# Row sends in growing groups, fewer side pieces ahead of two key operations, and an earlier load of the experts' first rows

## The chip, the cores and the metric

One core of a Trainium2 chip runs the whole program in one launch. The metric is the device time of an execution in microseconds (us). The engines are TensorE (PE; its weight loads are PEld), VectorE (DVE), ScalarE (ACT), GpSimd (POOL) and SyncE (SP, which here only issues transfers).

## The reference, cut to what matters

The model has two layers, each an attention followed by a mixture-of-experts block; x is 4 sequences of 1024 tokens of width 128.

```python
x = x + attn_a(layernorm(x))    # 16 heads of 64, softmax kernel features, then an ELU network of 512
x = x + ffn(layernorm(x))       # 160 experts, 8 for each token, inner width 64, and a shared expert
x = x + attn_b(layernorm(x))    # 16 heads of 8, causal
x = x + ffn(layernorm(x))

# inside attn_a: linear attention by random features
dash = einsum('bnhd,md->bnhm', data * dn, proj)
diag = sum(square(data), -1, keepdims=True) * dn * dn / 2
f    = ratio * (exp(dash - diag - max) + 1e-6)     # max per token (queries) or over all (keys)
kv   = einsum('bnhm,bnhd->bhmd', kf, v)

# inside ffn
top_w, top_idx = top_k(sigmoid(x @ router + bias), 8)
routed = sum over the 8 experts of weight * down(silu(gate(x)))
```

## The kernel before

**Order of the work.** A pass for the largest key comes first, then `attn_a` for the batches b = 0 to 3, each 1024 tokens in 8 tiles of 128 (TPB = 8). In the profile b = 1 runs from about 243 to 435 us, b = 2 to 640, b = 3 to 833. Then come the ELU network of batch 3 (`ffn_a`, f3), the routing of its tokens (`route`, m3, from 872 us), the experts of the first layer (`experts`, m, 926 to 1282), layer b, the last routing (`route`, n3, from 2248) and the experts of the second layer (`experts`, n, from 2302 to the end).

**A key tile of `attn_a`.** TensorE projects the keys of the tile (`psA`), their dash (`psB`, line 1020 for queries and its sibling for keys) and the values (line 992). ScalarE squares the keys (`a__sq`, line 1132), GpSimd adds the halves of the squares (`a__fold`, `fold_key_squares`, line 949), VectorE reduces them to `a__shift` (`key_square_sums`, line 804) and subtracts that from the dash into `a__arg` (`key_argument`, line 811), ScalarE takes the exponential, TensorE adds kf·v up. The eight query tiles follow: `query_peak` (line 815), `query_argument` (lines 820 and 826), and others.

**Side work on VectorE.** While batch b is in its attention, VectorE also finishes the network of batch b-1 and routes its tokens. That side work is a generator of pieces: first the ELU network's end and the norm of the expert input (lines 378 to 403; line 403 writes `g_xs`, the rows that go to the experts), then the router's scores, ranks and slots (up to line 659). `side(t, phase, count)` runs the next `count` pieces at three places of key tile t, by a table of numbers:

```python
for t in range(TPB):
    side(t, 0, PIECES[t][0])
    key_square_sums(t)
    side(t, 1, PIECES[t][1])
    key_argument(t)
    side(t, 2, PIECES[t][2])
```

**Side work on GpSimd.** Each token's row goes to a slot of each of its 8 experts in DRAM (`slots_in`), by one indirect transfer for 128 rows (line 1473): 64 for a batch. In batch b >= 2 the rows of batch b-2 leave: 46 in the key loop and some around it. GpSimd's queue runs in program order, so the fold of key tile t+1 stands behind all sends of tile t. In front of b = 2's and 3's loop some of the 64 were sent already, and in both kernels the key loop's sends end with the last of that batch.

**Side work on SyncE.** The route block before an experts block loads chunks of the experts' weights (`wgd`, line 1542, 3840 KB each: two chunks in m3, four in n3). The experts block then waits until the rows of the half's two batches have landed (`S.scattered`) and loads its first four groups of rows (`rows`, 256 KB each, DEEP = 4, line 1920). TensorE's first operation there turns these rows (line 1978). The buffer `rows` belongs to the experts block.

## Time and profile before

| what | value |
|---|---|
| time, median of 3 executions | 2839.03 us (2836.64 to 2840.02) |
| the profiled execution's own time | 2871.99 us |
| its span, first to last instruction | 2871.3 us |
| TensorE busy | 2020.4 us, 70% of the span |
| VectorE busy | 1647.2 us, 57% |
| ScalarE busy | 1083.0 us, 38% |
| GpSimd busy | 1349.4 us, 47% |
| mean granted clock of TensorE | 0.789 of full speed |

The profiled execution is 33 us longer than the median. Busy shares are means over stages with different limits: no engine is full over the span, so the stages that the change touches have to be read one by one.

### The profile page before, as it was taken

What the parts mean: (1) busy time and instruction counts of PE and PEld (TensorE: products, weight loads), DVE (VectorE), ACT (ScalarE), POOL (GpSimd) and SP (SyncE); (2) the same over time, 40 slices, a digit from 0 to 9 for tenths busy, and PEclk for the clock granted to TensorE, in tenths of its full rate; (3) what the DMA queues carried; (4) which work ended last, traced back from release to release, by engine and by line L of the source; (5) the groups of instructions that cost most, each with busy time, mean ns of one, the idle gap of its engine ahead of it and who ended that gap; (6) DMA issues with size and microseconds to landing.
All of it is one profiled execution on the core that took longest, in us unless ns stands there. A gap on an engine that the chain in (4) does not pass through costs nothing. (4 is left out here: it accounts for less than half of the span.)

```text
span 2871.3 us, 44772 instructions
## 1 busy us (share of the span) xinstructions
PE 2020.4 (70%) x15403; PEld 1129.8 (39%) x15403; DVE 1647.2 (57%) x4701; ACT 1083.0 (38%) x2067; POOL 1349.4 (47%) x1372
## 2 busy tenths in 40 slices
PE   5898887887883775665887889888888467766000
PEld 3456455455461554541332333333332255545000
DVE  5457585775777231456776778778783533145222
ACT  0263453444541443340545543443444144443000
POOL 0043166566673444553445531641554444355775
PEclk9899989889995887775777877876876589787555
DMA  9200001000034664554131121121100656565221
GB/s 370 96 1 4 1 6 34 23 11 33 20 130 155 192 206 155 180 180 121 28 88 48 46 76 25 53 69 36 49 29 25 250 179 207 176 188 174 70 60 44
DMA packets 132471, 275.63 MB, mean 96 GB/s; under 512 B 29411, under 2 KB 44387, under 8 KB 127891
## 3 DMA queue, kind: packets, MB, share of 16 engines
q1 hardware_dynamic: 99478, 205.60, 21.7%
q0 software_dynamic: 32768, 67.17, 7.7%
q8 instruction: 124, 2.03, 0.3%
q14 instruction: 101, 0.83, 0.1%
HBM read 146.34 MB, written 125.93 MB: 95 GB/s over the span
## 5 line engine op out<-in xcount | busy, mean ns | idle before, releaser
L1473 POOL DMA_INDIRECT slots_in<-g_xs,g_place x512 | 510.1, 996 | 373.0 <-issue 122.7
L2518 ACT ACTIVATE b_pT<-b_psE 128x512 f32<-128x512 f32 (+3 forms) x768 | 325.6, 491 | 449.6 <-PE b_psE L2415 392.6
L2271 DVE TENSOR_REDUCE b_peak<-b_psM 128x1 f32<-128x512 f32 (+3 forms) x768 | 395.1, 551 | 148.6 <-PE b_psM L2403 91.3
L1498 POOL DMA_INDIRECT r_xs<-slots_out,g_place x336 | 333.3, 992 | 237.2 <-ACT b_pT L2518 98.3
L2400 PE MATMUL b_psM<-b_kS,b_qS 72*128 72x512 bf16 (+3 forms) x768 | 290.1, 412 | 60.6 <-DVE b_peak L2271 29.7
L2415 PE MATMUL b_psE<-b_qS,b_kS 75*128 75x512 bf16 (+3 forms) x768 | 250.5, 402 | 45.0 <-ACT b_pT L2518 38.6
L1498 POOL DMA_INDIRECT g_xs<-slots_out,g_place x176 | 173.0, 983 | 126.1 <-issue 48.0
L2060 DVE COPY m_staged_w<-wgd 128x192 f32 x512 | 98.3, 264 | 230.0 <-PE m_psY L2002 165.7
L2427 PE MATMUL b_psV<-b_pT,b_vb 128*32 128x512 f32 (+3 forms) x1536 | 205.8, 616 | 30.8 <-POOL b_pT L2582 29.5
L2060 DVE COPY n_staged_w<-wgd 128x192 f32 x512 | 97.5, 263 | 216.0 <-PE n_psY L2002 118.6
L2400 PEld LDWEIGHTS b_psM<-b_kS,b_qS 72*128 72x128 bf16 x768 | 84.5, 112 | 263.7 <-DVE b_peak L2271 151.6
L2582 POOL TENSOR_SCALAR_AFFINE_SELECT b_pT<-b_pT 128x512 f32<-128x512 f32 x128 | 82.8, 647 | 219.8 <-ACT b_pT L2518 217.3
L2415 PEld LDWEIGHTS b_psE<-b_qS,b_kS 75*128 75x128 bf16 x768 | 77.0, 112 | 169.3 <-ACT b_pT L2518 98.0
L2403 PE MATMUL b_psM<-b_mask_q,b_ident_bf 128*128 128x128 bf16 x512 | 133.1, 260 | 0.0
L949 POOL TENSOR_TENSOR a__fold<-a__sq 128x512 f32<-128x512 f32 x32 | 40.6, 1270 | 179.5 <-ACT a__sq L1132 179.5
L1978 PE MATMUL m_psX<-g_ident,m_rows 128*128 128x128 f32 x416 | 84.3, 336 | 35.4 <-DMA m_rows<-slots_in 33.9
L1978 PE MATMUL n_psX<-g_ident,n_rows 128*128 128x128 f32 x416 | 84.6, 336 | 24.5 <-DMA n_rows<-slots_in 22.9
L992 PE MATMUL a__psB<-a_wv,a_xnT 128*128 128x512 f32 x128 | 73.1, 654 | 39.5 <-ACT a__v L1151 36.4
L2035 ACT ACTIVATE n_y<-n_psY 128x512 f32<-128x512 f32 x104 | 62.5, 602 | 77.2 <-DMA b_kS<-one_rows 44.2
L2035 ACT ACTIVATE m_y<-m_psY 128x512 f32<-128x512 f32 x104 | 62.4, 601 | 73.5 <-remote 37.3
L2023 ACT ACTIVATE m_xT<-m_psX 128x512 f32<-128x512 f32 x104 | 62.0, 596 | 69.9 <-issue 35.0
L1020 PE MATMUL a__psB<-a_wqp,a_xnT 128*128 128x512 f32 x128 | 70.5, 678 | 24.5 <-DVE a__arg L811 12.7
(639 smaller groups left out, 4167.9 us busy)
## 6 DMA issues: line engine op xcount, KB each, us to landing
wgd<-in_w_gdT SPq DMA_DIRECT2D x8, 3840.0 KB, 22.7
slots_in<-g_xs SPq DMA_DIRECT2D x26, 1024.0 KB
m_rows<-slots_in SPq DMA_DIRECT2D x104, 256.0 KB
slots_out<-m_y SPq DMA_DIRECT2D x104, 256.0 KB
n_rows<-slots_in SPq DMA_DIRECT2D x104, 256.0 KB
slots_out<-n_y SPq DMA_DIRECT2D x104, 256.0 KB
b_qS<-q_parts SPq DMA_DIRECT2D x48, 192.0 KB
b_kS<-k_parts SPq DMA_DIRECT2D x48, 192.0 KB
```

The costliest lines, as they stand in the source:

```text
L1473: self.nc.gpsimd.indirect_dma_start(self.G.slots_in[self.h], bass.IndirectOffsetOnAxis(self.G.place[:, TPH * self.h + t, k:k + 1], 0), sel ...
L1498: self.nc.gpsimd.indirect_dma_start(self.rows(i)[:, k, :], None, self.G.slots_out[t // TPH], bass.IndirectOffsetOnAxis(self.G.place[:, t, ...
L1978: last = nc.tensor.transpose(psX[:, n % 2, j * P:(j + 1) * P], rows[:, n % DEEP, j, :], G.ident[:])
L2035: nc.scalar.activation(y[:, n % DEEP, :, :].rearrange("p (q j) d -> p j q d", j=2), psY[:, n % 2, :, 0:2 * DM].rearrange("p j (q d) -> p j ...
L2060: last = nc.vector.tensor_copy(staged_w[:, d % STAGED, j, :], G.wgd[:].rearrange("p e i -> p (e i)")[:, bass.ds(e[j] * (INTER + DM), INTER ...
L2271: nc.vector.reduce_max(to, taking()[:, 0:size], AX.X).then_inc(m_taken, 1)
L2400: last = nc.tensor.matmul(ps[:, 0:n], qS[0:STACK, g, h, qt * P:(qt + 1) * P], kS[0:STACK, g, h, kh * HALF:kh * HALF + n], start=True, stop ...
L2403: last = nc.tensor.matmul(ps[:, n - P:n], ident_bf[:], mask_q[:], start=False, stop=True, skip_group_check=True)
L2415: nc.tensor.matmul(psE[:, j % BANKS, q0:HALF], kS[0:STACK + 3, g, h, kt * P:(kt + 1) * P], qS[0:STACK + 3, g, h, half * HALF + q0:(half + ...
L2427: last = nc.tensor.matmul(psV[32 * h:32 * h + 32, half, q0:HALF], vb[:, kt, g * HG + h, :], pT[:, e % KEPT, h, q0:HALF], start=(kt == 0), ...
L2518: nc.scalar.activation(pT[:, e % KEPT, h, q0:HALF], psE[:, j % BANKS, q0:HALF], ACT.Exp, scale=SCALE).then_inc(e_taken, 1)
L2582: nc.gpsimd.affine_select(out=tile, in_=tile, compare_op=ALU.is_ge, fill=0.0, base=0, pattern=[[0, HG], [1, P]], channel_multiplier=-1).th ...
```

## The change

It has three parts. The number of sends behind the fold of a key tile becomes a table, 2, 3, 6, 7, 7, 7, 7, 7, in place of 5 for each tile and 6 more at tile 0; both give 46. The table `PIECES` gets other numbers at key tiles 1, 2 and 7, for b = 1, 2 and 3. The buffer of the experts' rows is allocated in the memory that encloses route and experts, and the first four groups are loaded in the route block, in front of the weights' chunks.

```diff
-SEND_A_KEY_TILE, SEND_A_QUERY_TILE, SEND_IN_FFN, SEND_IN_ROUTE = 5, 2, 6, 5
+SEND_A_KEY_TILE = (2, 3, 6, 7, 7, 7, 7, 7)
+SEND_A_QUERY_TILE, SEND_IN_FFN, SEND_IN_ROUTE = 2, 6, 5
...
-    PIECES = ((3, 2, 5), (5, 2, 5), (3, 1, 3), (3, 1, 3), (2, 2, 4)) + 3 * ((5, 3, 6),)
+    PIECES = ((3, 2, 5), (3, 2, 6), (4, 1, 3), (3, 1, 3), (2, 2, 4), (5, 3, 6), (5, 3, 6), (4, 1, 6))
...
                 fold_key_squares(t)
-                if b >= 2 and t == 0:
-                    scatters[(b - 2) // BPH](SEND_IN_FFN)
                 if b >= 2:
-                    scatters[(b - 2) // BPH].of_batch(b - 2)(SEND_A_KEY_TILE)
+                    scatters[(b - 2) // BPH].of_batch(b - 2)(SEND_A_KEY_TILE[t])
...
+def expert_rows(m, S):
+    S.rows = m.sbuf("expert_rows", [P, DEEP, TURNS, DM])
+    S.rows_landed = [m.sem(f"rows_landed{i}") for i in range(DEEP)]
...
-def expert_loads(G, W, S, chunks):
+def expert_loads(G, W, S, chunks, first_rows=False):
     def loads(sp):
+        if first_rows:
+            for b in range(BPH):
+                sp.wait_ge(S.scattered[b], 16 * TPB * TOPK)
+            for i in range(DEEP):
+                load_rows(G, S, sp, 0, i)
         for c in chunks:
...
-        rows = m.sbuf("rows", [P, DEEP, TURNS, DM])
+        rows, rows_landed = S.rows, S.rows_landed
...
-                for b in range(BPH * h, BPH * (h + 1)):
-                    sp.wait_ge(S.scattered[b], 16 * TPB * TOPK)
-                for i in range(DEEP):
-                    load(h, i)
+                if h:
+                    for b in range(BPH * h, BPH * (h + 1)):
+                        sp.wait_ge(S.scattered[b], 16 * TPB * TOPK)
+                    for i in range(DEEP):
+                        load_rows(G, S, sp, h, i)
...
-                route(nc, "m3_", G, W, *part(BATCH - 1), send, expert_loads(G, W, S["m"], range(CHUNKS // 2)))
+                expert_rows(w2, S["m"])
+                route(nc, "m3_", G, W, *part(BATCH - 1), send, expert_loads(G, W, S["m"], range(CHUNKS // 2), True))
...
+                expert_rows(w3, S["n"])
...
-                      expert_loads(G, W, S["n"], range(CHUNKS)))
+                      expert_loads(G, W, S["n"], range(CHUNKS), True))
```

In the rows of the changed kernel the line numbers of `attn_a` up to the sends are larger by one (line 804 is 805 there), and the sends' line 1473 is 1472. The folds of a batch are counted here from 0, as the key tiles.

GpSimd's order in the key loop of b = 2, before; L949 is the fold of a key tile, L1473 a group of row sends, the number behind x how many.

```order
L949 TENSOR_TENSOR a__fold<-a__sq 128x512
L1473 DMA slots_in<-g_xs,g_place 26624x128 x11
L949 TENSOR_TENSOR a__fold<-a__sq 128x512
L1473 DMA slots_in<-g_xs,g_place 26624x128 x5
L949 TENSOR_TENSOR a__fold<-a__sq 128x512
L1473 DMA slots_in<-g_xs,g_place 26624x128 x5
L949 TENSOR_TENSOR a__fold<-a__sq 128x512
L1473 DMA slots_in<-g_xs,g_place 26624x128 x5
L949 TENSOR_TENSOR a__fold<-a__sq 128x512
L1473 DMA slots_in<-g_xs,g_place 26624x128 x5
```

The same place in the changed kernel.

```order
L950 TENSOR_TENSOR a__fold<-a__sq 128x512
L1472 DMA slots_in<-g_xs,g_place 26624x128 x2
L950 TENSOR_TENSOR a__fold<-a__sq 128x512
L1472 DMA slots_in<-g_xs,g_place 26624x128 x3
L950 TENSOR_TENSOR a__fold<-a__sq 128x512
L1472 DMA slots_in<-g_xs,g_place 26624x128 x6
L950 TENSOR_TENSOR a__fold<-a__sq 128x512
L1472 DMA slots_in<-g_xs,g_place 26624x128 x7
L950 TENSOR_TENSOR a__fold<-a__sq 128x512
L1472 DMA slots_in<-g_xs,g_place 26624x128 x7
```

The fold of key tile 1 stands behind 2 sends where it stood behind 11; the folds of tiles 4 to 7 stand behind 7 where they stood behind 5.

VectorE's order at key tile 1 of b = 2, before; L393 to L397 are one step of the norm's inverse root, L403 writes four tiles of the experts' rows, L436 copies what was picked before. In b = 1 a constant (L438) stands in its place.

```order
L393 TENSOR_TENSOR a_var<-a_rstd 128x8
L395 TENSOR_TENSOR a_var<-a_var,a_half 128x8
L397 SCALAR_TENSOR_TENSOR a_rstd<-a_var,a_rstd 128x8
L403 TENSOR_SCALAR g_xs<-g_x,a_mv,a_rstd 128x128 x4
L804 TENSOR_REDUCE a__shift<-a__fold 128x16
L403 TENSOR_SCALAR g_xs<-g_x,a_mv,a_rstd 128x128 x4
L436 COPY a__qsT<-o_picked_before 128x160
L811 TENSOR_TENSOR a__arg<-a__psB,a__shift 128x1024
L804 TENSOR_REDUCE a__shift<-a__fold 128x16
```

The same place in the changed kernel.

```order
L805 TENSOR_REDUCE a__shift<-a__fold 128x16
L394 TENSOR_TENSOR a_var<-a_rstd 128x8
L396 TENSOR_TENSOR a_var<-a_var,a_half 128x8
L398 SCALAR_TENSOR_TENSOR a_rstd<-a_var,a_rstd 128x8
L404 TENSOR_SCALAR g_xs<-g_x,a_mv,a_rstd 128x128 x4
L812 TENSOR_TENSOR a__arg<-a__psB,a__shift 128x1024
L404 TENSOR_SCALAR g_xs<-g_x,a_mv,a_rstd 128x128 x4
L437 COPY a__qsT<-o_picked_before 128x160
L805 TENSOR_REDUCE a__shift<-a__fold 128x16
```

The reduction of tile 1 (L805) stands one step of the root and four rows' tiles earlier, its argument (L812) in front of the second half of the rows; what is passed over comes behind, and from key tile 2 on the order is as before.

VectorE's order at key tile 7 of b = 2, before; L587 to L597 are operations of 128x1280 on the ranks, L601 the largest eight.

```order
L587 TENSOR_TENSOR a__beyond<-a__beyond,a__delta 128x1280
L804 TENSOR_REDUCE a__shift<-a__fold 128x16
L590 SCALAR_TENSOR_TENSOR a__logits<-a__probs,o_old_delta 128x1280
L594 TENSOR_TENSOR a__logits<-a__logits,a__beyond 128x1280
L597 TENSOR_TENSOR a__probs<-a__probs,a__logits 128x1280
L811 TENSOR_TENSOR a__arg<-a__psB,a__shift 128x1024
L601 MAX a__top<-a__probs 128x8 x8
```

The same place in the changed kernel.

```order
L805 TENSOR_REDUCE a__shift<-a__fold 128x16
L588 TENSOR_TENSOR a__beyond<-a__beyond,a__delta 128x1280
L812 TENSOR_TENSOR a__arg<-a__psB,a__shift 128x1024
L591 SCALAR_TENSOR_TENSOR a__logits<-a__probs,o_old_delta 128x1280
L595 TENSOR_TENSOR a__logits<-a__logits,a__beyond 128x1280
L598 TENSOR_TENSOR a__probs<-a__probs,a__logits 128x1280
L602 MAX a__top<-a__probs 128x8 x8
```

The reduction stands one piece earlier, the argument three. In b = 1 and 3 the pieces that it passes are parts of L601 and the short operations behind it.

VectorE's order a little later in b = 2, before; L643 to L656 compute slots and weights, L815 to L826 are the peak and the argument of query tile 0, L884 is a copy of kf·v.

```order
L640 TENSOR_SCALAR g_place<-a__slot_i 128x64
L643 TENSOR_SCALAR a__slot_i<-a__slot_i 128x64
L644 TENSOR_TENSOR g_place<-g_place,a__low 128x64
L646 TENSOR_TENSOR g_place<-g_place,a__slot_i 128x64
L653 TENSOR_TENSOR a__logits<-a__expert_i,a__index 128x8x64
L656 TENSOR_TENSOR a__logits<-a__logits,g_w 128x8x64
L815 TENSOR_REDUCE a__fold<-a__psB 128x16
L820 TENSOR_REDUCE a__shift<-a__fold 128x16
L826 TENSOR_TENSOR a__arg<-a__psB,a__shift 128x1024
L659 TENSOR_REDUCE g_w<-a__logits 128x64
L884 COPY a__vk<-a__psC 65x1024
```

The same place in the changed kernel.

```order
L641 TENSOR_SCALAR g_place<-a__slot_i 128x64
L816 TENSOR_REDUCE a__fold<-a__psB 128x16
L821 TENSOR_REDUCE a__shift<-a__fold 128x16
L827 TENSOR_TENSOR a__arg<-a__psB,a__shift 128x1024
L644 TENSOR_SCALAR a__slot_i<-a__slot_i 128x64
L645 TENSOR_TENSOR g_place<-g_place,a__low 128x64
L647 TENSOR_TENSOR g_place<-g_place,a__slot_i 128x64
L654 TENSOR_TENSOR a__logits<-a__expert_i,a__index 128x8x64
L657 TENSOR_TENSOR a__logits<-a__logits,g_w 128x8x64
L885 COPY a__vk<-a__psC 65x1024
L816 TENSOR_REDUCE a__fold<-a__psB 128x16
```

Here L644 to L657 (L643 to L656 before) follow the operations of query tile 0 instead of standing in front of them, and L659 goes behind query tile 1. In b = 1 and 3 the same pieces stand in front of query tile 0 in both kernels.

## Rows read from the trace of the kernel before

**Rows 1.** The page's costliest groups: all row sends, busy us, mean ns | idle before

```profile
L1473 POOL DMA_INDIRECT slots_in<-g_xs,g_place x512 | 510.1, 996 | 373.0 <-issue 122.7
```

**Rows 2.** The waits, 430 to 840 us: total, times, longest

```profile
DVE a__shift L804 <- POOL a__fold L949: 40.9, 7, 8.9
```

**Rows 3.** VectorE's timeline, b = 2: start us, duration us, instruction, [idle before <-releaser]

```profile
469.52 1.22 DVE L811 TENSOR_TENSOR a__arg<-a__psB,a__shift 128x1024 f32<-128x1024 f32 x1
...
478.99 1.51 DVE L393 TENSOR_TENSOR a_var<-a_rstd 128x8 f32<-128x8 f32 x1 [2.29 <-issue]
...
485.79 1.22 DVE L811 TENSOR_TENSOR a__arg<-a__psB,a__shift 128x1024 f32<-128x1024 f32 x1
```

**Rows 4.** VectorE's timeline, b = 1, key tiles 0 and 1

```profile
278.14 1.23 DVE L811 TENSOR_TENSOR a__arg<-a__psB,a__shift 128x1024 f32<-128x1024 f32 x1
...
289.57 1.12 DVE L403 TENSOR_SCALAR g_xs<-g_x,a_mv,a_rstd 128x128 f32<-128x128 f32 x4
...
290.69 1.16 DVE L811 TENSOR_TENSOR a__arg<-a__psB,a__shift 128x1024 f32<-128x1024 f32 x1
```

**Rows 5.** VectorE's timeline, b = 3, key tiles 0 and 1

```profile
675.58 1.23 DVE L811 TENSOR_TENSOR a__arg<-a__psB,a__shift 128x1024 f32<-128x1024 f32 x1
...
692.16 1.16 DVE L811 TENSOR_TENSOR a__arg<-a__psB,a__shift 128x1024 f32<-128x1024 f32 x1
```

**Rows 6.** GpSimd's timeline, b = 2, key loop

```profile
512.72 1.27 POOL L949 TENSOR_TENSOR a__fold<-a__sq 128x512 f32<-128x512 f32 x1 [2.48 <-ACT a__sq L1132]
...
522.46 1.26 POOL L949 TENSOR_TENSOR a__fold<-a__sq 128x512 f32<-128x512 f32 x1 [2.30 <-ACT a__sq L1132]
...
544.07 1.27 POOL L949 TENSOR_TENSOR a__fold<-a__sq 128x512 f32<-128x512 f32 x1 [3.53 <-ACT a__sq L1132]
...
550.22 2.04 POOL L1473 DMA_INDIRECT slots_in<-g_xs,g_place  x1 [0.30 <-issue]
```

**Rows 7.** GpSimd's timeline, b = 3, key tiles 4 and 5

```profile
719.96 1.27 POOL L949 TENSOR_TENSOR a__fold<-a__sq 128x512 f32<-128x512 f32 x1 [2.46 <-ACT a__sq L1132]
...
729.22 1.27 POOL L949 TENSOR_TENSOR a__fold<-a__sq 128x512 f32<-128x512 f32 x1 [1.77 <-ACT a__sq L1132]
```

**Rows 8.** VectorE's timeline, b = 2, key tile 5

```profile
523.76 0.69 DVE L804 TENSOR_REDUCE a__shift<-a__fold 128x16 f32<-128x512 f32 x1
```

**Rows 9.** VectorE's timeline, b = 2, before the first query tile

```profile
560.92 0.63 DVE L643 TENSOR_SCALAR a__slot_i<-a__slot_i 128x64 int32<-128x64 int32 x1
...
563.63 1.23 DVE L815 TENSOR_REDUCE a__fold<-a__psB 128x16 f32<-128x1024 f32 x1
```

**Rows 10.** SyncE's queue, start of both experts blocks

```profile
925.67 4.97 SPq L1920 DMA_DIRECT2D m_rows<-slots_in  x5
...
2302.14 4.11 SPq L1920 DMA_DIRECT2D n_rows<-slots_in  x5
```

**Rows 11.** TensorE's timeline, first operation of both experts blocks

```profile
929.18 1.12 PE L1978 MATMUL m_psX<-g_ident,m_rows 128*128 128x128 f32 x4 [18.21 <-DMA m_rows<-slots_in]
...
2304.77 1.12 PE L1978 MATMUL n_psX<-g_ident,n_rows 128*128 128x128 f32 x4 [17.34 <-DMA n_rows<-slots_in]
```

**Rows 12.** TensorE's timeline, query projections, b = 2 and b = 3

```profile
566.74 3.78 PE L1020 MATMUL a__psB<-a_wqp,a_xnT 128*128 128x512 f32 x4 [3.49 <-DVE a__arg L826]
...
581.34 2.80 PE L1020 MATMUL a__psB<-a_wqp,a_xnT 128*128 128x512 f32 x4
...
767.58 1.98 PE L1020 MATMUL a__psB<-a_wqp,a_xnT 128*128 128x512 f32 x4
...
775.12 1.88 PE L1020 MATMUL a__psB<-a_wqp,a_xnT 128*128 128x512 f32 x4
```

**Rows 13.** Windows: busy PE, PEld, DVE, ACT, POOL; PEclk, DMA share, GB/s

```profile
556.00:583.00 27.00, 23.51 (x86) 11.71 (x87) 14.31 (x30) 9.97 (x10) 6.62 (x6) 0.63 0.00 1
...
2280.00:2290.00 10.00, 2.67 (x13) 0.89 (x11) 8.75 (x32) 0.00 (x0) 2.38 (x3) 0.50 1.02 423
...
2290.00:2300.00 10.00, 0.00 (x0) 0.00 (x0) 9.05 (x26) 0.00 (x0) 0.00 (x0) 0.50 0.22 85
```

More of the change, by code:

```diff
@@ L1535, in add, with load_rows @@
         self.add_half(dve, i)
-def expert_loads(G, W, S, chunks):
-    def loads(sp):
+def expert_rows(m, S):
+    S.rows = m.sbuf("expert_rows", [P, DEEP, TURNS, DM])
+    S.rows_landed = [m.sem(f"rows_landed{i}") for i in range(DEEP)]
+def load_rows(G, S, sp, h, i):
+    n = h * HALF_GROUPS + i
+    src = G.slots_in[h].rearrange("(g p j) d -> g p (j d)", p=P, j=TURNS)
+    sp.dma_start(S.rows[:, n % DEEP, :, :].rearrange("p j d -> p (j d)"), src[group_order()[i][0]]).then_inc(S.rows_landed[n % DEEP], 16)
+def expert_loads(G, W, S, chunks, first_rows=False):
+    def loads(sp):
+        if first_rows:
[3 more added lines that the diff above has]
+                load_rows(G, S, sp, 0, i)
         for c in chunks:
@@ L1906, in experts @@
         flat = "p j d -> p (j d)"
-        src, dst = ([s.rearrange("(g p j) d -> g p (j d)", p=P, j=TURNS) for s in slots] for slots in (G.slots_in, G.slots_out))
+        dst = [s.rearrange("(g p j) d -> g p (j d)", p=P, j=TURNS) for s in G.slots_out]
         order = group_order()
         dynamic_at = [i for i, (_, d) in enumerate(order) if d is not None]
-        rows_landed = [m.sem(f"rows_landed{i}") for i in range(DEEP)]
         stored = [m.sem(f"stored{i}") for i in range(DEEP)]
@@ L1917, in _ @@
         def _(sp):
-            def load(h, i):
-                n = h * HALF_GROUPS + i
-                sp.dma_start(rows[:, n % DEEP, :, :].rearrange(flat), src[h][order[i][0]]).then_inc(rows_landed[n % DEEP], 16)
             def store(h, i):
@@ L1934, in _ @@
                         sp.wait_ge(x_turned, h * HALF_GROUPS + i + 1)
-                        load(h, i + DEEP)
+                        load_rows(G, S, sp, h, i + DEEP)
                     store(h, i)
```

## The prediction, made before the changed kernel ran

> **What bounds the kernel now.** I read the page's busy shares first: no engine is full over the span, so a mean says little. Then I read the waits of the stretch 430 to 840 us, the two batches in which rows leave. VectorE waits there for GpSimd's fold of the key squares seven times, 40.9 us in all and 8.9 us at most [rows 2]. But a fold that comes last is mostly one that waited for ScalarE's squares, and these hang on the tile before; where the fold comes right after ScalarE's squares (2.48 us of waiting for them before one fold [rows 6]), GpSimd has slack. So I went through the timelines tile by tile. A key tile is a ring: VectorE's argument, ScalarE's exponential, TensorE's products and the next tile's squares, the fold, VectorE's reduction. Where VectorE has side work between two arguments, that side work sets the length of the tile. At key tile 1 it does: VectorE is occupied from the argument of tile 0 to that of tile 1, for 485.79 - 469.52 = 16.27 us in b = 2 [rows 3], 692.16 - 675.58 = 16.58 us in b = 3 [rows 5], but 290.69 - 278.14 = 12.55 us in b = 1, which has the same side work and no sends [rows 4]. The excess of 3.72 and 4.03 us is what I charge to the sends. Part of it can be seen: VectorE's small multiplication of 128x8 starts after 2.29 us of idleness that no awaited result explains, and takes 1.51 us itself [rows 3].
>
> The last read was the start of the two experts blocks. SyncE issues the first loads of rows at 925.67 and 2302.14 [rows 10], and TensorE's first operation starts at 929.18 and 2304.77, released by that load [rows 11]. Nothing else is late there: this load is on the path for 3.5 and 2.6 us.
>
> **Key tile 1.** All four rows' tiles of line 403 in the second group, 1.12 us in b = 1 [rows 4], stand in front of the argument and now come behind it. VectorE is occupied without a break there, so the argument comes 1.1 us earlier, and the pieces passed over fall into the time in which VectorE later waits for the fold [rows 2]. In b = 1 that is all: -1.1 (bounds 0 and -1.1).
>
> In b = 2 and 3 the same 1.1 us count, and the sends thin out beside VectorE's short operations: 11 sends and then 5 stood behind folds 0 and 1, now 2 and 3. I take 0.6 of the excess, since 5 of 16 sends stay but the fold now falls into the same stretch. That gives 1.1 + 0.6 x 3.72 = 3.3 for b = 2 and 1.1 + 0.6 x 4.03 = 3.5 for b = 3. The bounds are the excess untouched (-1.1 each) and all of it gone (-4.8 and -5.1).
>
> **The later tiles.** The sends that left tile 0 go to tiles 2 to 7. One costs 0.996 us [rows 1] and 0.30 us between two [rows 6]. Seven with a fold of 1.27 take 7 x 1.296 + 1.27 = 10.3 us. The folds of tiles 4 and 5 stand 522.46 - 512.72 = 9.7 us apart in b = 2 [rows 6] and 729.22 - 719.96 = 9.3 in b = 3 [rows 7]; VectorE's reduction of tile 5 starts at 523.76, right at the end of the fold [rows 8], so this fold is on the path. It slips by 0.6 and 1.1 us, together +1.7. The three periods from fold 4 to fold 7 take 544.07 - 512.72 = 31.35 us, 10.45 each [rows 6], so the others hold seven sends with 0.1 us to spare. The bounds are 0 (the ring has a microsecond of slack elsewhere) and +5 (six folds late by 0.5 to 0.8 more, sends at 1.1 us).
>
> That slack is small, so what a send costs decides. One of tile 7 took 2.04 us [rows 6], twice the mean. The Trainium skill speaks against larger groups here: SBUF — State Buffer, "SBUF: two separate sides", says that a VectorE operation in a two-port mode locks GpSimd out of writing the descriptors of such a transfer. By the same page ("Who interferes with whom") an operation with two inputs from SBUF takes only the read side, and so should not slow a send. If every send of a group of seven went as that longest one, a group with its fold would take 7 x 2.34 + 1.27 = 17.7 us instead of 10.3. The mean of 512 sends is 0.996, so I keep that.
>
> **Key tile 7.** In b = 2 three pieces that start at 560.92 stand in front of the first query peak at 563.63 [rows 9]: 2.7 us of VectorE's time that now come behind it. A fourth (line 659) goes behind query tile 1, some 0.7 us by the like reduction of line 804 [rows 8], and half of that counts. I take -3.0, bounds 0 (TensorE's query projection, at half clock, ends no earlier) and -3.8. In b = 1 and 3 the argument comes earlier, but VectorE's work in front of the query peak stays the same: 0, at best -2 for both, since only short waits can go.
>
> **The experts' rows.** Both routing blocks last over 50 us, and the loads are now issued at their start, far ahead of their use. They need the rows of batches 0 and 1 of the half only, and these have left before. What is left of 3.5 and 2.6 us is a small wait for VectorE's staging and the entry of the block; I keep 0.3 each and take -3.2 and -2.3, together -5.5 (bounds 0 and -6.1). The cost: 1 MB more moves in front of the weights. While n's weights come down, 423 GB/s move from 2280 to 2290 and only 85 from 2290 to 2300 [rows 13]: at the first rate 1 MB takes 2.5 us, and the weights, down by 85/423 of the second stretch or 2292, would be down by 2294.5, 7.6 us before the block. m loads half as much in a block of the same length. That cover hides the 1 MB; without it each block would pay the 2.5 us.
>
> **TensorE's clock.** Four projections of the query tiles take 3.78 us in b = 2 at one place and 1.98 and 1.88 in b = 3 [rows 12]; the granted clock of b = 2's stretch is 0.63 of full speed [rows 13], so it runs there mostly at the lower level (1.2 GHz), and b = 3, in half the time for the same four, at the upper (2.4 GHz). From the second to the third group of projections it is 581.34 - 566.74 = 14.6 us in b = 2 and 775.12 - 767.58 = 7.5 us in b = 3 [rows 12]. The edit at tile 7 moves TensorE's idle time just in front of this, in all three batches. I can't tell which way, and take 0; b = 2 could win 7 us, and b = 1 and 3 could lose up to 7 each.
>
> **The sum.** -1.1 - 3.3 - 3.5 + 1.7 - 3.0 - 5.5 = -14.7 us. Against the profiled execution's 2871.99 that is 2857.3. The median of the runs shown is 2839.03, 33 us less, and the edits are worth the same there: 2824.3, so 2824.
>
> **Rivals.**
> - The forecast: chance 0.55, its own range 2818 to 2830.
> - The stalls stay, only moved: the sends hit other operations of VectorE, and the fold of tile 1 now falls on its short operations. Then tile 1 gives 3.3, tile 7 and the rows 8.5, the later tiles cost 3: -9, 2830. For it speaks that the total of sends is the same; against it that b = 1 is 4 us shorter. Chance 0.15.
> - The clock is lost: TensorE idles longer in front of the query tiles and goes through them at the lower level in b = 1 and 3. That costs up to 14 us by the two intervals above; I price it at 11, 2835. That b = 2 has just this speaks for it; that b = 3 has a wait there too and keeps its clock, against. Chance 0.13.
> - The clock is won: b = 2 goes through at the upper level, -7, and b = 1 a little, -3: 2814. Chance 0.10.
> - The other side, GpSimd becomes the bound of key tiles 3 to 7. A group fits into 10.45 us up to a mean send of (10.45 - 1.27)/7 - 0.30 = 1.01 us, just above today's. Above it each 0.1 us costs 0.7 us on four folds of two batches, 5.6 us. At 1.29 us the gain is gone, and at 1.4 the kernel is 22 - 15 = 7 us slower, 2846. The send of 2.04 us speaks for it; the mean of 0.996 over all stages against. The page's rule of the two-port lock is this rival's ground. Chance 0.07.
>
> **How the numbers follow.** A measurement of this kernel can tell about 0.2%, 5.7 us, from no change, so faster ends at 2833.3. Faster are the forecast (0.55), the moved stalls (0.12 of 0.15) and the won clock (0.10): 0.77. The same are the lost clock (0.13) and what is left of the moved stalls (0.03): 0.16. Slower is the last rival: 0.07. The range 2811 to 2835 leaves out that rival, half of the lost clock and a little on the low side.
>
> **What the changed profile would show.** The interval between the arguments of tiles 0 and 1 at about 11.4, 13.0 and 13.1 us in b = 1, 2, 3. Folds 4 and 5 some 10.3 us apart. The first query peak of b = 2 about 2.7 us sooner behind the reduction of key tile 7. TensorE's first operation of both experts blocks within 0.5 us of the block's start. The forecast is wrong if the mean send in the key loop is above 1.1 us, if folds stop waiting for ScalarE from tile 3 on, if the query stretches show a clock near one half, or if the experts' first operation still waits, for its weights or for staging.

## The result, and the profile after

The change made the kernel slower: 2852.67 us (median of 16 executions, 2841.49 to 2866.03) against 2845.97 us (16 executions) before, a ratio of 1.0029 with a 95% interval of 1.0016 to 1.0043, some 8 us where 15 us less were forecast. The profiled execution took 2848.53 us. It is shorter than that of before only because that one, 2871.99 us, is longer than every other execution of its kernel on record (the next is 2861.88); below, a second profile of the kernel before (e1, span 2847.0 us) stands for it.

The page of the changed kernel: its span, and the group of all row sends (as in [rows 1]).

```profile
span 2846.8 us, 44776 instructions
...
L1472 POOL DMA_INDIRECT slots_in<-g_xs,g_place x512 | 509.7, 996 | 360.2 <-issue 119.2
```

A send costs 996 ns on average as before, so the rival that made each send dearer was not what happened. Three places answer to the prediction.

The first rows of the experts, SyncE's queue and TensorE's timeline (as in [rows 10, 11]):

```profile
878.40 1.93 SPq L1547 DMA_DIRECT2D w_expert_rows<-slots_in  x4
...
880.38 0.91 SPq L1559 DMA_DIRECT2D wgd<-in_w_gdT  x2
...
929.84 1.09 PE L1991 MATMUL m_psX<-g_ident,w_expert_rows 128*128 128x128 f32 x4 [14.69 <-PEq L96]
...
2288.97 1.08 PE L1991 MATMUL n_psX<-g_ident,w_expert_rows 128*128 128x128 f32 x4 [14.70 <-PEq L96]
```

The four loads are issued at 878.40, 51 us ahead of use. TensorE's first operation no longer waits for them; what ended its wait is its own sequencer at the entry of the block.

Key tiles 0 and 1 of b = 2 on VectorE (as in [rows 3]):

```profile
470.52 1.23 DVE L812 TENSOR_TENSOR a__arg<-a__psB,a__shift 128x1024 f32<-128x1024 f32 x1
...
478.98 0.68 DVE L805 TENSOR_REDUCE a__shift<-a__fold 128x16 f32<-128x512 f32 x1
...
481.70 1.22 DVE L812 TENSOR_TENSOR a__arg<-a__psB,a__shift 128x1024 f32<-128x1024 f32 x1
```

From argument to argument it is 481.70 - 470.52 = 11.2 us (16.3 before; 11.4 in b = 3, 11.0 in b = 1). This part went further than forecast.

Key tile 5 of b = 3, in the order TensorE (values, line 991), ScalarE (exponential and values, lines 1137 and 1150), GpSimd (folds 5 and 6 and the last of seven sends between them) and VectorE (reduction of tile 6):

```profile
727.01 1.08 PE L991 MATMUL a__psB<-a_wv,a_xnT 128*128 128x512 f32 x2
...
733.38 1.13 PE L991 MATMUL a__psB<-a_wv,a_xnT 128*128 128x512 f32 x2 [3.57 <-ACT a__v L1150]
...
726.21 1.15 ACT L1137 ACTIVATE a__qe<-a__arg,a_ngmax 128x1024 f32<-128x1024 f32 x1 [3.19 <-DVE a__arg L812]
...
732.73 0.60 ACT L1150 ACTIVATE a__v<-a__psB 128x512 f32<-128x512 f32 x1 [5.37 <-remote]
...
721.07 1.29 POOL L950 TENSOR_TENSOR a__fold<-a__sq 128x512 f32<-128x512 f32 x1
...
730.27 0.98 POOL L1472 DMA_INDIRECT slots_in<-g_xs,g_place  x1 [0.30 <-issue]
...
734.33 1.26 POOL L950 TENSOR_TENSOR a__fold<-a__sq 128x512 f32<-128x512 f32 x1 [3.08 <-ACT a__sq L1131]
...
735.62 0.69 DVE L805 TENSOR_REDUCE a__shift<-a__fold 128x16 f32<-128x512 f32 x1 [4.11 <-POOL a__fold L950]
```

The product of the values starts at 727.01 and takes 1.1 us. ScalarE needs it (and the tile's kf·v, which ends at 727.2) and is free from 727.4, but starts at 732.73, 4.6 us later, released by something that the profile can't name. Then the squares, the fold at 734.33 and VectorE's reduction at 735.62 are late one after the other. The trace's updates of semaphores, the counters by which an engine tells the others that work is done, say more: those of the last kf·v product, of the values and of the next key projection, which should have come between 727.2 and 729.8, come together at 732.65 to 732.75, 0.1 to 0.3 us behind the landing of the group's last send (732.33 to 732.51). So the matmuls started in time, and their completion reached the others late, in one burst. I call this a held completion. The profile takes the starts of matmuls from the chip and models their ends, so it can't tell whether a matmul ended late or only the word of it came late.

The query tiles of b = 3 on TensorE (as in [rows 12]):

```profile
754.77 1.99 PE L1019 MATMUL a__psB<-a_wqp,a_xnT 128*128 128x512 f32 x4 [1.32 <-DVE a__arg L812]
...
766.29 3.78 PE L1019 MATMUL a__psB<-a_wqp,a_xnT 128*128 128x512 f32 x4 [5.28 <-DVE a__arg L827]
...
780.89 2.70 PE L1019 MATMUL a__psB<-a_wqp,a_xnT 128*128 128x512 f32 x4
```

The first projection now waits 1.3 us and runs at full clock (1.99 us), the second waits 5.3 us and takes 3.78 us, and the third group stands 14.6 us behind it, as b = 2 had before; in b = 3 this was 7.5 us. The granted clock from 766 to 781 us is 0.50, the lower level.

All profiles can be laid side by side by the start times of VectorE's reductions of key tiles 0 to 7 (line 804 or 805) and of its first three query peaks (815 or 816): intervals in us, worked out from the timelines, for the kernel before (e1), the sends alone (e2), the pieces alone (e3) and the change.

```
kernel, batch   0-1   1-2   2-3   3-4   4-5   5-6   6-7   7-peak0  peak0-1 peak1-2
e1_same    1   13.5   7.0  10.7  10.7   9.5   9.9  18.1   8.1   6.2  10.8
e1_same    2   17.0   7.7  12.0  10.7   9.5  10.0  15.0  14.5   6.8   9.1
e1_same    3   17.2   7.9  12.5  10.7   9.5  10.0  15.1   8.1   5.6   7.4
e2_sends   1   13.5   7.0  12.2  10.7   9.5   9.9  15.1   8.1   5.6   9.1
e2_sends   2   13.3   7.1  12.1  10.8  10.0  13.3  21.7  14.5   6.4   9.5
e2_sends   3   13.6   7.0  12.5  10.9  10.1  13.3  17.4   8.1   5.5  10.8
e3_pieces  1   11.3   7.8  11.0  10.8   9.5   9.9  14.2  10.2   6.9  13.0
e3_pieces  2   15.4   9.9  12.0  10.7   9.5  10.0  13.4  13.7   6.9  13.5
e3_pieces  3   14.7  10.5  12.5  10.8   9.5  10.0  14.1  10.6   6.9  13.3
after      1   11.3   7.8  11.0  10.7   9.5   9.9  14.1  10.2   6.9  13.0
after      2   11.4   7.9  12.0  10.8  10.0  13.4  15.0  15.3   6.9   9.4
after      3   11.4   8.1  13.9  10.9  10.1  13.2  16.2  11.4   6.9  13.5
```

### The profile page after: what moved, and what is told of

Same layout as the page of the kernel before. It is cut to its first block and busy times, and to the rows that moved or that the text cites. A ratio compares the mean times of both kernels' runs of the same rounds, so it can differ in the third digit from the quotient of the medians.

```text
span 2846.8 us, 44776 instructions
## 1 busy us (share of the span) xinstructions
PE 1987.9 (70%) x15403; PEld 1114.7 (39%) x15403; DVE 1647.2 (58%) x4701; ACT 1083.5 (38%) x2067; POOL 1346.3 (47%) x1372
## 5 line engine op out<-in xcount | busy, mean ns | idle before, releaser
L2413 PE MATMUL b_psM<-b_kS,b_qS 72*128 72x512 bf16 (+3 forms) x768 | 280.4, 396 | 69.5 <-DVE b_peak L2284 36.9
L2428 PE MATMUL b_psE<-b_qS,b_kS 75*128 75x512 bf16 (+3 forms) x768 | 239.6, 388 | 50.8 <-ACT b_pT L2531 47.1
L1991 PE MATMUL m_psX<-g_ident,w_expert_rows 128*128 128x128 f32 x416 | 82.9, 332 | 30.5 <-DMA w_expert_rows<-slots_in 15.4
L1991 PE MATMUL n_psX<-g_ident,w_expert_rows 128*128 128x128 f32 x416 | 80.8, 326 | 19.6 <-PEq L96 14.7
L932 POOL TENSOR_TENSOR a__prod<-a__qe,a__ksum 128x1024 f32<-128x1024 f32 x32 | 76.3, 2383 | 36.8 <-ACT a__ksum L1239 33.5
```

Of the source, the lines that this page charges most:

```text
L1991: last = nc.tensor.transpose(psX[:, n % 2, j * P:(j + 1) * P], rows[:, n % DEEP, j, :], G.ident[:])
L2413: last = nc.tensor.matmul(ps[:, 0:n], qS[0:STACK, g, h, qt * P:(qt + 1) * P], kS[0:STACK, g, h, kh * HALF:kh * HALF + n], start=True, stop ...
L2428: nc.tensor.matmul(psE[:, j % BANKS, q0:HALF], kS[0:STACK + 3, g, h, kt * P:(kt + 1) * P], qS[0:STACK + 3, g, h, half * HALF + q0:(half + ...
```

## The experiments

The runs met chips of two kinds. On the first (the result above, e1 to e4, e16, e17) the kernel before takes 2843 to 2846 us, on the second (e5 to e15) 2664 to 2666 us. Ratios are always against the kernel before on the same chip. In the stretch 243 to 833 us, not one of some 325 semaphore updates of TensorE's matmuls comes more than 1 us behind its matmul in the profiles of the second kind. In each profile of the first kind it is 28 to 42 of some 320, if the next record of the semaphore is taken for each. Some of these are only missing records, since the engine that waited had gone on long before; but 8 to 23 of them come in bursts with others, and where the waiting engine starts right behind such a burst, as in the rows above, the lateness is real. In b = 1, whose key loop has no sends, the profiles of e1 and of the change have none.

**e1, the kernel before again.** No edit.

> The kernel before, unchanged, as a control. Its ratio to itself should be 1.000 within 0.15%, which tells how far a single comparison can be off. Its profile should have a span near 2846 us instead of the 2871.3 of the first one; the lengths of the key tiles in b = 1, 2 and 3 should repeat to 0.3 us (16.3 to 16.6 us between the arguments of key tiles 0 and 1 in b = 2 and 3), while layer b and the second experts block, which the change does not touch, should come out some 10 and 7 us shorter than in the first profile, by the granted clock. If instead the key tiles differ by more than 1 us between the two profiles of the same kernel, no reading of a single tile can carry the explanation.

Ratio 1.0000 (0.9986 to 1.0015). Key tiles repeat to 0.5 us between the two profiles of this kernel, but the second interval between peaks of b = 2 was 13.6 us in the first and 9.1 in this one, and tile 6 of b = 1 takes 18.1 us in some profiles and 15.1 in others: single intervals of tile 6 and behind it can't be read to better than that. Layer b kept its 954.3 us, against what I expected; the second experts block was shorter by 7.6 us.

**e2, the sends alone.**

```diff
-SEND_A_KEY_TILE, SEND_A_QUERY_TILE, SEND_IN_FFN, SEND_IN_ROUTE = 5, 2, 6, 5
+SEND_A_KEY_TILE = (2, 3, 6, 7, 7, 7, 7, 7)
...
-                if b >= 2 and t == 0:
-                    scatters[(b - 2) // BPH](SEND_IN_FFN)
-                    scatters[(b - 2) // BPH].of_batch(b - 2)(SEND_A_KEY_TILE)
+                    scatters[(b - 2) // BPH].of_batch(b - 2)(SEND_A_KEY_TILE[t])
```

> Only the sends' table (2, 3, 6, 7, 7, 7, 7, 7), the pieces and the rows as before. Theory A (groups hold TensorE's completions): the reduction of key tile 1 comes about 13 us behind that of tile 0 in b = 2 and 3 instead of 17.4 and 17.6, so 8 to 9 us are won there, but key tile 5 takes 13.3 us instead of 10.1 to 10.4, tiles 2, 4 and 6 up to 1 us more each, and the time is between 4 us better and 4 us worse than before. Theory B (the pieces do the harm): the sends alone win 6 to 8 us and key tile 5 stays near 10.5 us. Theory C (GpSimd's queue alone, 10.3 us for a group and a fold): tile 5 is 10.5 us, and the time 5 us better.

1.0031 (1.0014 to 1.0047), 9 us worse, beyond the 4 us that theory A allowed. Tile 0 wins 3.7 and 3.6 us in b = 2 and 3, and tile 5 takes 13.3 us in both, as theory A said; tile 6 gives back another 6.7 and 2.4. By tile 5, theory C, which had GpSimd's queue alone, falls, and so does theory B, by which the sends alone would win.

**e3, the pieces alone.**

```diff
-    PIECES = ((3, 2, 5), (5, 2, 5), (3, 1, 3), (3, 1, 3), (2, 2, 4)) + 3 * ((5, 3, 6),)
+    PIECES = ((3, 2, 5), (3, 2, 6), (4, 1, 3), (3, 1, 3), (2, 2, 4), (5, 3, 6), (5, 3, 6), (4, 1, 6))
```

> Only the table of pieces, sends and rows as before. Theory A: in b = 1 the tile 1 is 2 us shorter and tile 7 of b = 2 some 3 us; tile 5 stays at 10 us in all batches; the time is 3 to 8 us better. Theory B: the time is worse by 4 us or more, from the query tiles of b = 1 and 3, where the third group of query projections comes 3 us later behind the first peak than before (18.7 instead of 15 us in b = 1 counted from the first to the third peak).

1.0043 (1.0023 to 1.0063), 12 us worse. Theory A said better, so it was wrong here: the pieces hurt by themselves, and at the place that theory B named, the query tiles of b = 1 and 3. In b = 2 and 3 key tile 1 gives back what tile 0 won.

**e4, the rows alone.** The diff of the change without its first two parts.

> Only the earlier load of the experts' rows. By the profile of the change: 3 us less between the route block's start and TensorE's first operation in each layer, of which 0.9 is given back before the first down projection, so 4 us better than before. Rival: the buffer or the longer queue costs something later in the experts blocks, then each of them is longer by 2 us or more from TensorE's first operation to its last, and the time is the same or worse.

0.9981 (0.9965 to 0.9998), 5 us better. From the route block to TensorE's first operation it is 53.4 instead of 57.1 us in m and 53.9 instead of 56.6 in n; 0.8 us of each come back before the first down projection. In the changed kernel's m this is ScalarE's second take of turned rows, which starts 0.9 us after TensorE's work on them (934.68 against 933.79). The rival falls. On the second kind of chip nothing comes back (6.7 us in e9 and e15, 6.8 in e6).

**e5, the pieces of tile 7 alone.**

```diff
-... (2, 2, 4)) + 3 * ((5, 3, 6),)
+... (2, 2, 4), (5, 3, 6), (5, 3, 6), (4, 1, 6))
```

> Only the pieces of key tile 7, (4, 1, 6) for (5, 3, 6). Theory A (TensorE's wait moves from ahead of query tile 0 to ahead of query tile 1, and the half clock then covers the products behind it): in b = 1 and 3 the stretch from the reduction of tile 7 to the first peak grows from 8.1 to 10.2 to 10.6 us, and the first two intervals between peaks from 5.6 + 7.4 (or 6.2 + 10.8) to 6.9 + 13.0 us; b = 2 wins 1 to 2 us; the time is 8 to 13 us worse than before, nearly all that the table of pieces cost as a whole (+12). Theory B (tile 1 and 2 did it): the time is within 3 us of before.

1.0044 (1.0022 to 1.0066), 12 us worse: all of the pieces' harm, and on the other kind of chip.

**e6, the pieces of tiles 1 and 2 alone.**

```diff
-    PIECES = ((3, 2, 5), (5, 2, 5), (3, 1, 3), ...
+    PIECES = ((3, 2, 5), (3, 2, 6), (4, 1, 3), ...
```

> Only the pieces of key tiles 1 and 2. Theory A: 1.3 us less in b = 1 over key tiles 0 to 3, and in b = 2 and 3 what tile 0 wins (1.5 to 2.5 us) tile 1 gives back, as the profile of the whole table of pieces showed; query tiles as before; the time is 0 to 3 us better. Theory B: the time is 8 us or more worse.

0.9984 (0.9962 to 1.0007): a gain of 4 us that is not beyond the interval. With e5 it settles where the pieces hurt. TensorE's projections of the query tiles in b = 3, first e6 (the second and third group), then e5 (the first three):

```profile
748.04 1.88 PE L1020 MATMUL a__psB<-a_wqp,a_xnT 128*128 128x512 f32 x4
...
758.25 2.00 PE L1020 MATMUL a__psB<-a_wqp,a_xnT 128*128 128x512 f32 x3
```

```profile
752.26 1.98 PE L1020 MATMUL a__psB<-a_wqp,a_xnT 128*128 128x512 f32 x4 [1.21 <-DVE a__arg L811]
...
763.03 3.78 PE L1020 MATMUL a__psB<-a_wqp,a_xnT 128*128 128x512 f32 x4 [4.53 <-DVE a__arg L826]
...
777.63 2.32 PE L1020 MATMUL a__psB<-a_wqp,a_xnT 128*128 128x512 f32 x4
```

In e5 the argument of key tile 7 comes earlier, so the first projection waits only 1.21 us; but VectorE has the same pieces left in front of the first peak, so the second projection waits 4.53 us for the query argument. It runs at half speed (3.78 us for four), and so does what follows. From the second group to the third it is 10.2 us in e6 and 14.6 in e5. The windows over these two stretches, e6 and then e5 (columns as in [rows 13]; the granted clock is the third number from the end):

```profile
748.00:758.00 10.00, 10.00 (x45) 5.33 (x44) 3.04 (x4) 5.17 (x5) 4.33 (x3) 0.73 0.01 2
```

```profile
763.00:777.00 14.00, 13.97 (x44) 7.01 (x45) 3.99 (x4) 4.25 (x4) 2.35 (x1) 0.50 0.00 1
```

All of e5's stretch is at the lower level (0.50, 1.2 GHz); e6's is at the upper for nearly half of it (0.73).

The same side by side on the second kind of chip:

```
kernel, batch   0-1   1-2   2-3   3-4   4-5   5-6   6-7   7-peak0  peak0-1 peak1-2
e6_tile1   1   11.3   7.8  11.0  10.7   9.6   9.9  15.1   8.1   5.5   9.1
e6_tile1   2   14.5   7.9  11.6  10.7   9.5   9.9  15.0  14.5   6.7  10.8
e6_tile1   3   14.5   8.1  11.4  10.7   9.6   9.9  15.1   8.1   6.4  10.8
e5_tile7   1   13.6   7.0  12.3  10.7   9.6   9.9  14.1  10.2   6.9  13.3
e5_tile7   2   14.9   7.1  11.8  10.7   9.5   9.9  13.4  13.7   6.9  13.4
e5_tile7   3   15.6   7.4  12.0  10.8   9.5   9.9  14.1  10.6   6.9  13.1
e9_change  1   11.3   7.8  11.0  10.8   9.6   9.9  14.1  10.2   6.9  12.9
e9_change  2   11.4   7.9  11.0  10.8  10.0  10.1  15.7  15.6   6.9   9.4
e9_change  3   11.3   8.1  12.0  10.9  10.1  10.2  17.2  11.4   6.8   9.1
e10_sends  1   13.5   7.0  12.3  10.7   9.5   9.9  15.1   8.1   5.6   7.4
e10_sends  2   13.3   7.1  11.9  10.8  10.0  10.2  17.2  14.5   6.6   9.3
e10_sends  3   13.7   7.0  11.3  10.9  10.1  10.2  18.1   8.1   5.6  10.8
```

From the reduction of tile 6 to the third peak e5 is longer than e6 by 6.7, 0.5 and 4.5 us in b = 1, 2 and 3, together 11.7 us. The timed runs gave e5 0.44% of 2664 us over the kernel before, which is 11.7 us too. That both agree to the tenth is partly luck: the interval is some 6 us either way, and the second interval between peaks differs by up to 3.3 us between profiles with the same pieces (7.4, 9.1 and 10.8 us).

**e7, e11, e13 and e16, groups of 6 and 8 at key tile 5.** The old sends, but 6 in b = 2 and 8 in b = 3 at key tile 5, taken from tile 7.

```diff
+SEND_A_KEY_TILE = {2: (11, 5, 5, 5, 5, 6, 5, 4), 3: (11, 5, 5, 5, 5, 8, 5, 2)}
```

> The sends as before, but at key tile 5 a group of 6 in b = 2 and of 8 in b = 3, taken from key tile 7 (4 and 2 there). It doses the group size at one place. Theory A (TensorE's completions come only with the landing of the group's last send, and ScalarE waits for them): from the reduction of tile 5 to that of tile 6 it is 11.5 to 12.5 us in b = 2 and 14.3 to 15 us in b = 3, against 10.0 with 5 sends and 13.3 with 7, so 1.27 us for each send. Theory C (GpSimd's queue alone): 10.0 us in b = 2 and 11.8 us in b = 3. The time as a whole is 3 to 8 us worse under A, 0 to 2 us worse under C.

> Groups of 6 (b = 2) and 8 (b = 3) sends at key tile 5, as in e7. Theory A': on a chip of the first kind key tile 5 takes 11.5 to 12.5 and 14.3 to 15 us, on one of the second kind 9.9 and 11.4 us again, where 8 sends and a fold take 11.4 us and so GpSimd's queue sets it. Rival: 9.9 and 11.4 us on both kinds, then the harm of e2 came from something other than the size of the group.

> As e7 and e11: 6 sends (b = 2) and 8 (b = 3) at key tile 5. If the profile shows late updates of TensorE's semaphores (before near 2846 us): theory A', the lag grows with the group, says 11.5 to 12.5 us for key tile 5 in b = 2 and 14.3 to 15 us in b = 3; the rival, that any group above 5 trips into a later step of about 3.3 us, says 13.3 in both; the rival that the size does not matter says 10.0 and 11.4 us. If it shows none (before near 2665 us): 9.9 and 11.4 us as before.

> As e13, one look. With late updates of TensorE's semaphores: 11.5 to 12.5 us for key tile 5 in b = 2 (6 sends) and 14.3 to 15 us in b = 3 (8 sends) if the lag lasts as long as the group; 13.3 in both if it is a step; 10.0 and 11.4 us if the size does not matter. Without late updates: 9.9 and 11.4 us.

e7, e11 and e13 met the second kind of chip: 9.9 and 11.4 us for tile 5 each time, ratios 1.0009, 1.0011 and 1.0010 (each interval holds 1). e16 met the first: 11.5 us with 6 sends and 14.2 us with 8, beside 10.0 with 5 (e1) and 13.3 with 7 (e2; both sizes gave the same in b = 2 and in b = 3). It has one execution only, 2860.51 us against a median of 2843.44, which tells nothing of the whole time. The size of the group sets tile 5 there, by 1.5, 1.8 and 0.9 us for each further send. The product of the values on TensorE and ScalarE's take of them, tile 5 of b = 2 and b = 3, first in e16:

```profile
526.94 1.08 PE L991 MATMUL a__psB<-a_wv,a_xnT 128*128 128x512 f32 x2
...
530.92 0.60 ACT L1150 ACTIVATE a__v<-a__psB 128x512 f32<-128x512 f32 x1 [3.63 <-remote]
...
728.31 1.08 PE L991 MATMUL a__psB<-a_wv,a_xnT 128*128 128x512 f32 x2
...
734.99 0.60 ACT L1150 ACTIVATE a__v<-a__psB 128x512 f32<-128x512 f32 x1 [6.33 <-remote]
```

The same rows in e13, on the second kind of chip:

```profile
520.40 1.08 PE L991 MATMUL a__psB<-a_wv,a_xnT 128*128 128x512 f32 x2
...
521.52 0.60 ACT L1150 ACTIVATE a__v<-a__psB 128x512 f32<-128x512 f32 x1 [0.77 <-PE a__psB L991]
...
720.66 1.08 PE L991 MATMUL a__psB<-a_wv,a_xnT 128*128 128x512 f32 x2
...
721.77 0.60 ACT L1150 ACTIVATE a__v<-a__psB 128x512 f32<-128x512 f32 x1 [0.77 <-PE a__psB L991]
```

From the product's start to ScalarE's it is 4.0 us behind 6 sends and 6.7 us behind 8 in e16, and 1.1 us both times in e13. The same stretch is 2.5 us behind 5 sends in e1, 5.8 us behind 7 in e2 (4.1 and 5.7 in the change), and 1.1 us in b = 1, whose key loop has no sends, on both kinds. Where completions are not held, 8 sends still cost 1.5 us at this tile, since GpSimd needs 11.4 us for them and the fold; there theory C's price (11.8) is nearly right.

**e8, e12, e14 and e17, a tuned table.** The change with large groups only at the tiles that last longer, and the old pieces at tile 7.

```diff
-SEND_A_KEY_TILE = (2, 3, 6, 7, 7, 7, 7, 7)
+SEND_A_KEY_TILE = (3, 4, 8, 7, 6, 5, 5, 8)
...
-... (2, 2, 4), (5, 3, 6), (5, 3, 6), (4, 1, 6))
+... (2, 2, 4)) + 3 * ((5, 3, 6),)
```

> The change with two numbers turned round: the sends are (3, 4, 8, 7, 6, 5, 5, 8), again 46, large groups only where the key tile lasts longer, and key tile 7 has its old pieces (5, 3, 6). Rows and pieces of tiles 1 and 2 as in the change. Theory A: tile 0 about 12 us in b = 2 and 3, tiles 4 to 6 as before (9.5, 10.0, 15), query tiles as before; 4 us less for the rows, 1.3 for b = 1, 4 to 5 us less in each of b = 2 and 3: 10 to 15 us better than before. If the harm of the change lies elsewhere, the time is not better than that of the rows alone (-5).

> The tuned variant of e8. Theory A': 0.6% better on a chip of the second kind, as there; on one of the first kind 0.3 to 0.5% better, since its larger groups at key tiles 2, 3 and 7 are held there. Rival: no better than the rows alone (-0.19%).

> As e8 and e12. With late updates: 0.3 to 0.5% better than before, and key tile 4 or 5 of b = 2 or 3 longer than on the other kind of chip by up to 2 us; without: 0.67% better again.

> As e14. With late updates 0.3 to 0.5% better than before; without, 0.6% better.

0.9933 (0.9910 to 0.9956), 0.9932 (0.9910 to 0.9954) and 0.9939 (0.9918 to 0.9960) on the second kind, 17 us better than before, and 0.9959 (0.9943 to 0.9976) on the first, 12 us better. It beats both kernels on both kinds. On the first, its groups of 8 and 7 at tiles 2 and 3 are held: these take 14.8 and 12.4 us in b = 2, against 12.0 and 10.7 in e1, so the table is not the best one there.

**e9 and e10, the change and the sends alone on the second kind of chip.**

> The whole change once more, beside the three kernels below on one chip. The chips differ: on that of e1 to e4 (before: 2846 us) TensorE's updates of its semaphores come up to 5.5 us after the matmul while rows leave, on that of e5 to e8 (before: 2664 us) the profile shows no such lag. Theory A' (the lag belongs to the chip, and the sends hurt only through it; the pieces of tile 7 hurt everywhere through the clock): on a chip of the first kind the change is 0.2 to 0.4% worse, on one of the second kind it is within 0.15% of before, since the pieces' +12 us are met by -5 for the rows and about -8 for sends and tile 1. Rival: the ratio is the same on both kinds.

> The sends' table alone, as in e2. Theory A': on a chip of the first kind 1.003 as in e2, with 13.3 us for key tile 5; on one of the second kind 0.997 to 0.9985 (4 to 8 us better), with key tile 5 at 10.3 us and key tile 0 at 13.3 instead of 15 us. Rival (GpSimd's queue or VectorE's stalls do the harm): worse on both, and tile 5 above 12 us on both.

The change is 0.9986 (0.9966 to 1.0006), and the sends alone are 1.0009 (0.9984 to 1.0033), not the gain that was expected: tile 0 wins some 1.8 us in b = 2 and 3 (13.3 and 13.7 against 15.1 and 15.6 in e7), but tile 6 takes 17.2 and 18.1 us, against 15.0 and 15.1 in e6. Yet e7, whose sends up to there are the old ones, has these same 17.2 and 18.1 us, so the longer tiles can't be charged to the sends. Tile 5 is 10.1 to 10.2 us in both, as GpSimd's 10.3 us for seven sends and a fold say (e15 has 10.2 and, once, 11.5).

**e15, the change with the old pieces at tile 7.** Only the second hunk of the tuned table's diff.

> The change with the old pieces at key tile 7, all else as in the change. By the tables of peaks: the pieces of tile 7 cost 7 to 9 us in each of b = 1 and 3 and win 1 to 2 in b = 2. With late updates: 0.3% better than before, against 0.29% worse for the change; without: 0.5% better, against 0.14% for the change. If the harm is in the sends alone, it stays within 0.1% of the change.

0.9954 (0.9932 to 0.9977) against 0.9986 for the change: these pieces are worth some 8.5 us within the change too, though the two intervals still overlap.

## Why the prediction was wrong

The forecast of 2824 us was 28.7 us too low. Of this 7 us are the base: the three executions of the kernel before that were known had a median of 2839.03 us, and sixteen have 2845.97. The other 22 us are terms of the sum.

- **Key tile 1** (-1.1, -3.3, -3.5, with what follows). Right in kind and too small: from argument to argument 12.5, 16.0 and 16.1 us (e1) became 11.0, 11.2 and 11.4. But 0.7 us come back at the next tile in b = 1 and 0.2 in b = 2 and 3. Net by the reductions: -1.5, -5.4, -5.6, a little beyond all three bounds. The 0.6 of the excess was too low: nearly all of it went. Not all of that excess was a stall of VectorE as the prediction had it: with the old sends it is 3.4 and 3.6 us in e1 and only 1.5 and 1.9 in e7, so part of it belongs to the kind of chip.
- **The experts' rows** (-5.5). Right: -5.4 by e4's ratio. That the 1 MB would hide behind 7.6 us of cover held; the 0.8 us given back in each block was not in the sum.
- **The later tiles** (+1.7, bounds 0 and +5). This is one of the two steps that failed in kind. The forecast took the slack from GpSimd's queue, "7 x 1.296 + 1.27 = 10.3 us", and on the second kind of chip that is what tile 5 takes (10.2). On the kind of chip of the result tiles 2 to 6 of b = 2 and 3 cost 10.5 us more than in e1 (4.1 and 6.4 by the first table), of which 3.4 and 3.2 are tile 5; that is twice the upper bound. What the sum lacked is that TensorE's completions come late there while a group leaves, and that a wait of ScalarE on TensorE behind the group is lengthened by it, so that the ring is late although GpSimd has room. A trace of it was there in the profile of the kernel before, ScalarE at tile 5 of b = 2, and was not looked at:

```profile
531.28 0.60 ACT L1151 ACTIVATE a__v<-a__psB 128x512 f32<-128x512 f32 x1 [2.56 <-remote]
```

- **TensorE's clock** (0, "I can't tell which way"). The other step that failed, and the larger one where completions are not held. The rows held the answer: VectorE's work in front of the first query peak stayed the same, as the prediction says of b = 1 and 3, so an earlier argument of key tile 7 would move TensorE's idle time from ahead of the first projection to ahead of the second, next to the products whose length the clock decides. The rival that named this had 0.13 and a price of +11; the pieces of tile 7 measured +11.7 (e5). The sign that the prediction had set for it, query stretches with a clock near one half, came true (0.50 in b = 3).
- **Key tile 7 of b = 2** (-3.0). Mis-sized, at +0.9: from the reduction of tile 7 to the second peak it is 22.2 us in the change and 21.3 in e1. In e5, without the sends, it is 20.6 against 21.2 in e6, so 0.6 was there to be had, with 1.6 more at tile 6. That the rest was TensorE's, whose projections at half clock end no earlier (the upper bound of the prediction), fits, but was not tested by itself.
- **The other side** was a rival with the right place and the wrong price. Key tiles 3 to 7 did become longer, but no send became dearer: 996 ns over all, and 1.06 and 1.02 us in the key loops of b = 2 and 3 against 1.05 and 1.04 in e1. (A few of 1.2 to 2.05 us lift these means; the seven between folds 4 and 5 below take 0.95 to 0.99 us each.) GpSimd was the bound in two tiles only, by its timeline of b = 2 in the changed kernel (folds 4 to 7):

```profile
508.39 1.28 POOL L950 TENSOR_TENSOR a__fold<-a__sq 128x512 f32<-128x512 f32 x1
...
518.43 1.29 POOL L950 TENSOR_TENSOR a__fold<-a__sq 128x512 f32<-128x512 f32 x1
...
531.87 1.27 POOL L950 TENSOR_TENSOR a__fold<-a__sq 128x512 f32<-128x512 f32 x1 [2.88 <-ACT a__sq L1131]
...
545.49 1.26 POOL L950 TENSOR_TENSOR a__fold<-a__sq 128x512 f32<-128x512 f32 x1 [3.43 <-ACT a__sq L1131]
```

  Folds 4 and 5 follow a send at once, and these tiles are 0.1 and 0.5 us longer than in e1; folds 6 and 7 waited 2.9 and 3.4 us for ScalarE. The Trainium skill's rule that a two-port VectorE operation starves a send's descriptors (SBUF — State Buffer, "SBUF: two separate sides") therefore priced nothing of the difference between the two kernels.
- **The sum.** On the first kind of chip the parts alone measured -5.4 (rows), +12.2 (pieces) and +8.8 (sends), 15.6 together, and the whole +8.3. The difference of 7 us is within what these four intervals allow (each some 5 us either way); about 3 us of it are tiles 0 and 1, where pieces and sends help each other: -3.7 and -4.3 us if e2 and e3 are added, -5.4 and -5.6 in the change (b = 2 and 3).

What stays open: what holds TensorE's completions beside a group of sends, and why on some chips only. No run here changed that itself. That the lag causes the long tile 5 rests on the dose (5, 6, 7 and 8 sends) and on the same kernel without lag and without the long tile on the other kind of chip, which differs in more than this; it was not taken away on one chip by itself. Nor is it known why tile 6 takes 15, 17 or 18 us in several runs of both kinds.

## What to carry to other kernels

Before work is taken from in front of an operation, ask where the wait that it ended will stand next: an idle time of TensorE that moves from ahead of short work to ahead of a chain of matmuls can cost the clock of the whole chain. Background transfers of one engine are not free for the others by that engine's queue alone; look at the unnamed waits beside them, and keep groups short where an engine waits for TensorE. And a table of numbers that shares out work is best judged entry by entry: of this change's parts one won 5 us, one lost 12, and one lost 9 on one kind of chip and nothing that can be told from noise on the other.

## What the runs showed of the hardware that was not expected

On one kind of chip TensorE's semaphore updates come late and in bursts beside indirect sends from GpSimd: at key tile 5, for the tile's last kf·v product, by 2.2 to 2.7 us with groups of 5, 3.7 with 6, 5.5 to 5.6 with 7 (4.2 in b = 2 of the change) and 6.4 with 8. Each of these bursts stands within 0.4 us of the landing of the group's last send, before or behind it; the starts of the matmuls are undisturbed. The Trainium skill says that TensorE never waits on anyone for a port of SBUF (SBUF — State Buffer, "Who interferes with whom"); the starts agree with that. Chips differ in this: none of 326 updates of the changed kernel was over 1 us late on the second kind (e9). On it the blocks of experts take 263 us instead of 349 (m) and 245 instead of 334 (n), from the first down projection to the last, for one and the same program, while its routing blocks and its key tiles of b = 1 are the same to 1%.
